# Last stage of a transformer block on Trainium2: second bias as matmul rows, shorter normalising passes, and the projection moved between turn and hidden layer

## What is computed

```python
x = x + conv_ref(_ln_c(x), Wq, bq, Wk, bk, Wv, bv, Wp, bp, rel_h, rel_w)   # attention; its last line is out @ Wp + bp
t = tokens(x)
t = t + ffn_ref(_ln_t(t), w1, b1, alpha_w1, alpha_a1, w2, b2, alpha_w2, alpha_a2)

def ffn_ref(x0, ...):
    xq = round(clip(x0 / alpha_a1.mean(), -8, 7))
    x1 = xq @ wq1.T * alpha_w1 * alpha_a1.mean() + b1
    x1 = clip(gelu(x1), -10, 10)
    hq = round(clip(x1 / alpha_a2.mean(), -8, 7))
    return hq @ wq2.T * alpha_w2 * alpha_a2.mean() + b2
```

## Time and profile before

| | us |
|---|---|
| median of 3 runs | 906.96 (906.38 to 907.9) |
| the profiled execution, its own time | 904.3 |
| span of its trace | 902.5 |
| busy in the span: TensorE | 791.0 (88%) |
| VectorE | 743.8 (82%) |
| ScalarE | 558.8 (62%) |
| POOL | 423.4 (47%) |
| mean granted TensorE clock, share of full speed | 0.949 |

### The profile page before, as it was taken

The page is one execution under the profiler, slowest core; times in us unless marked ns, Lnnn a source line. Parts: engine busy times, 40 slices in busy tenths (PEclk is TensorE's granted clock), DMA queues, the critical chain, the costliest instruction groups (busy, mean ns, idle before and its releaser), DMA issues. The chain is left out here.

```text
span 902.5 us, 15297 instructions
## 1 busy us (share of the span) xinstructions
PE 791.0 (88%) x5848; PEld 407.7 (45%) x5848; DVE 743.8 (82%) x1493; ACT 558.8 (62%) x609; POOL 423.4 (47%) x263
## 2 busy tenths in 40 slices
PE   5899554479999999999999999999999999678874
PEld 2555454134444444444444444444444442256653
DVE  6998855498989988988998999998888894069995
ACT  1333345027777777777777777777777778447773
POOL 3777794436364454637263735445373324112220
PEclk9999788589999999999999999999999999889986
DMA  7676599999439392948567493939395000433411
GB/s 193 212 226 206 164 300 374 256 194 208 90 88 188 77 200 60 205 85 190 111 147 154 109 191 74 198 68 201 63 206 96 13 12 12 134 105 123 140 36 53
DMA packets 65675, 130.06 MB, mean 144 GB/s; under 512 B 9465, under 2 KB 45306, under 8 KB 57146
## 3 DMA queue, kind: packets, MB, share of 16 engines
q1 hardware_dynamic: 57634, 115.95, 56.2%
q10 hardware_dynamic: 7968, 13.13, 4.2%
HBM read 89.73 MB, written 34.60 MB: 138 GB/s over the span
## 5 line engine op out<-in xcount | busy, mean ns | idle before, releaser
L1065 DVE TENSOR_REDUCE at_piece_neg<-at_r_ps 128x1 f32<-128x512 f32 x768 | 482.8, 682 | 68.1 <-PE at_r_ps L935 64.7
L1028 ACT ACTIVATE at_probs<-at_s_ps 128x1024 f32<-128x1024 f32 x384 | 371.9, 1021 | 130.6 <-PE at_s_ps L956 129.3
L935 PE MATMUL at_r_ps<-op_mix_k,op_mix_q 128*128 128x256 f16 (+1 forms) x1920 | 282.0, 257 | 29.9 <-DMA op_mix_q<-bias_parts 17.8
L935 PEld LDWEIGHTS at_r_ps<-op_mix_k,op_mix_q 128*128 128x128 f16 x1920 | 148.2, 98 | 295.1 <-DVE at_piece_neg L1065 194.1
L850 POOL COPY op_mix_q<-op_mix_q 2x4096 f16<-2x4096 f16 x48 | 172.6, 3596 | 231.0 <-ACT op_mix_q L1033 230.5
L956 PE MATMUL at_s_ps<-op_mix_q,op_mix_k 128*128 128x512 f16 x768 | 227.7, 380 | 1.1 <-ACT at_probs L1028 0.5
L970 PE MATMUL at_o_ps<-at_probs,op_v_u 128*32 128x512 f32 x1536 | 204.2, 604 | 0.0
L218 POOL MEMSET op_mix_q<- 2x10240 f32 x12 | 103.5, 8627 | 0.6
L1033 ACT ACTIVATE op_mix_q<-at_r_ps 2x1024 f16<-2x1024 f16 x48 | 48.5, 1011 | 60.7 <-PE at_r_ps L946 60.7
L956 PEld LDWEIGHTS at_s_ps<-op_mix_q,op_mix_k 128*128 128x128 f16 x768 | 73.4, 98 | 19.6 <-ACT at_probs L1028 10.7
L854 POOL TENSOR_TENSOR at_o_sb<-at_o_sb,at_inv_rows 128x512 f32<-128x512 f32 x24 | 30.7, 1280 | 86.2 <-DVE at_inv_rows L1092 86.2
(11 more groups left out here) (121 smaller groups left out, 674.4 us busy)
## 6 DMA issues: line engine op xcount, KB each, us to landing
op_mix_q<-qk_parts SPq DMA_DIRECT2D x48, 640.0 KB, 10.7
op_mix_q<-bias_parts SPq DMA_DIRECT2D x120, 120.0 KB, 10.3
op_mix_q<-bias_parts SPq DMA_DIRECT2D x72, 128.0 KB, 10.3
bias_parts<-op_mix_q ACTq DMA_DIRECT2D x8, 1024.0 KB, 13.1
qk_parts<-op_mix_q SPq DMA_DIRECT2D x24, 256.0 KB, 2.3
v_rows<-pr_v_st SPq DMA_DIRECT2D x8, 768.0 KB, 4.1
op_mix_k<-qk_parts SPq DMA_DIRECT2D x48, 128.0 KB, 13.1
op_v_u<-v_rows SPq DMA_DIRECT2D x12, 512.0 KB, 14.2
```

The lines of the kernel that those rows point to most:

```text
L935: last = pe.matmul(r_bank("piece", at)[:, first % GROUP:first % GROUP + n], mix_q[owner.buf][:, variant, j, qt * P:(qt + 1) * P], mix_k[ow ...
L1028: act.activation(probs[n % PRING][:, 2 * pair:2 * pair + 2, :], s_ps[pair][:, :, :], ACT.Exp).then_inc(exp_done, 1)
L1065: dve.tensor_reduce(piece_neg[half][:, i:i + 1], r_bank("piece", at)[:, :], AX_X, ALU.max, negate=True).then_inc(reduced, 1)
```

## The change

1. b2 is no longer added by VectorE. In `scales` it is divided by s2, split into three bf16 parts (high part, then the rest twice), and these go to rows 0, 32 and 64 of b2_parts, a bf16 tile of 96 rows, zero elsewhere. In `second` one more matmul per tile, a tile of ones against b2_parts, opens each sum in f_ps. `add_b2` and y_b go; b2 is loaded by `Weights.load`. y now has a ring of four buffers, and `residual` waits until the result four groups back is made.
2. `normalise`: POOL makes r0 * inv_a1 (r3) behind the power, and the third small operation takes it, so that y_n comes out divided by the activation's step. y_r is then (y_n + MAGIC) min (MAGIC + 7), and y_q is (y_r max (MAGIC - 8)) - MAGIC; y_i goes. The memset ahead of the statistics goes too.
3. `stage_c` scales all four tiles in one pass.
4. TensorE's `hidden` is split into `turn` and `hidden`, and the queue order is turn(g), project(g+2), hidden(g), second(g-1).

The diff, without the places that only pass b2 on:

```diff
-        self.dram = (w1, aw1, aa1, w2, aw2, aw2_cols, aa2)
+        self.dram = (w1, aw1, aa1, w2, aw2, aw2_cols, aa2, b2)
+        self.b2_parts = self.sb("b2_parts", [3 * SLOT, C], BF16)
+        self.ones = self.sb("ones", [3 * SLOT, P], BF16)
...
-        area, lens = ops.weight_area, (HT * C, HID, C, HT, HT)
+        area, lens = ops.weight_area, (HT * C, HID, C, HT, HT, C, C)
...
-        self.aa2_row, self.aa1_row, self.aw1_sb, self.inv_w1 = places[1:5]
+        self.aa2_row, self.aa1_row, self.aw1_sb, self.inv_w1, self.b2_row, self.inv_s2 = places[1:7]
+        self.b2_high = self.inv_s2.bitcast(BF16)[:, 0:C]
...
     def load(self, sp):
-        w1, aw1, aa1, w2, aw2, aw2_cols, aa2 = self.dram
...
+                         (self.aa1_row[:, :], aa1.partition_broadcast(P)), (self.aa2_row[:, :], aa2.partition_broadcast(P)),
+                         (self.b2_row[:, :], b2.partition_broadcast(P))):
             sp.dma_start(dst, src).then_inc(self.params_in, 16)
...
         step, link = self.step, lambda ins: self.chain(dve, ins)
-        dve.wait_ge(self.params_in, 16 * 7)
+        dve.wait_ge(self.params_in, 16 * 8)
         link(dve.reciprocal(self.inv_w1[:, :], self.aw1_sb[:, :]))
         link(dve.reciprocal(self.inv_w2[:, :], self.aw2_sb[:, :]))
         link(dve.tensor_reduce(step[:, 0:1], self.aa1_row[:, :], AX_X, ALU.add))
...
+        link(dve.memset(self.b2_parts[:, :], 0.0))
+        link(dve.memset(self.ones[:, :], 1.0))
+        link(dve.reciprocal(self.inv_s2[:, :], self.s2_row[:, :]))
+        link(dve.tensor_tensor(self.b2_row[:, :], self.b2_row[:, :], self.inv_s2[:, :], ALU.mult))
+        for i in range(3):
+            row = slice(i * SLOT, i * SLOT + 1)
+            link(dve.tensor_scalar(self.b2_high[:, :], self.b2_row[:, :], 1.0, None, ALU.mult))
+            link(dve.tensor_scalar(self.b2_parts[row, :], self.b2_high[row, :], 1.0, None, ALU.mult))
+            if i < 2:
+                link(dve.tensor_tensor(self.b2_row[:, :], self.b2_row[:, :], self.b2_high[:, :], ALU.subtract))
 
         for at, edge, limit, op in ((0, 10.0, QP, ALU.min), (1, -10.0, QN, ALU.max)):
             link(dve.tensor_scalar(self.bound[:, at:at + 1], self.inv_a2, edge, MAGIC, ALU.mult, ALU.add))
...
+    YRING = 4
...
-        y = [ph.sb(f"y{s}", [P, TILES, C], F32) for s in range(2)]
-        y_b = [ph.sb(f"y_b{s}", [P, TILES, C], F32) for s in range(2)]
+        y = [ph.sb(f"y{s}", [P, TILES, C], F32) for s in range(YRING)]
...
+        rstd = [ph.sb(f"rstd{s}", [P, 4, TILES], F32) for s in range(2)]
...
-        y_i = ph.sb("y_i", [P, TILES, C], BF16)
...
+                pool.wait_ge(pow_done, g.n + 1)
+                pool.tensor_tensor(out=rstd[g.s][:, 3, :], in0=rstd[g.s][:, 0, :], in1=wt.inv_a1.to_broadcast([P, TILES]), op=ALU.mult).then_inc(scaled_pow, 1)
 
             inverse_std(FIRST)
             inverse_std(FIRST.after(1))
...
-                st, mv, rs = stats[g.s], meanvar[g.s], rstd[g.s]
+                st, mv, y_g = stats[g.s], meanvar[g.s], y[g.n % YRING]
                 dve.wait_ge(x_loaded[g.s], (g.it + 1) * 16)
                 dve.wait_ge(proj_done, g.n + 1)
-                dve.tensor_tensor(y[g.s][:, :, :], p_ps[:, :, 0:C], x_in[g.s][:, :, :], ALU.add).then_inc(y_done, 1)
+                need(dve, res_done, g.n - YRING + 1)
+                dve.tensor_tensor(y_g[:, :, :], p_ps[:, :, 0:C], x_in[g.s][:, :, :], ALU.add).then_inc(y_done, 1)
                 dve.wait_ge(y_done, g.n + 1)
                 for t in range(TILES):
-                    last = dve.bn_stats(st[:, t, :], y[g.s][:, t, :])
+                    last = dve.bn_stats(st[:, t, :], y_g[:, t, :])
                 last.then_inc(stats_done, 1)
                 dve.wait_ge(stats_done, g.n + 1)
-                dve.memset(rs[:, 1, :], 0.0)
                 for t in range(TILES):
                     last = dve.bn_aggr(mv[:, t, :], st[:, t, :])
...
-                r0, r1, r2 = (rs[:, i, :] for i in range(3))
+                r0, r1, r2, r3 = (rs[:, i, :] for i in range(4))
                 dve.tensor_tensor(r1, r0, r0, ALU.mult).then_inc(newton, 1)
                 dve.wait_ge(newton, g.n * 3 + 1)
                 dve.scalar_tensor_tensor(out=r2, in0=r1, scalar=-0.5, in1=var_eps[g.s][:, :], op0=ALU.mult, op1=ALU.mult).then_inc(newton, 1)
                 dve.wait_ge(newton, g.n * 3 + 2)
-                dve.scalar_tensor_tensor(out=r1, in0=r2, scalar=1.5, in1=r0, op0=ALU.add, op1=ALU.mult).then_inc(newton, 1)
+                dve.wait_ge(scaled_pow, g.n + 1)
+                dve.scalar_tensor_tensor(out=r1, in0=r2, scalar=1.5, in1=r3, op0=ALU.add, op1=ALU.mult).then_inc(newton, 1)
                 dve.wait_ge(newton, g.n * 3 + 3)
                 for t in range(TILES):
-                    last = dve.tensor_scalar(y_n[:, t, :], y[g.s][:, t, :], mv[:, t, 0:1], rs[:, 1, t:t + 1], ALU.subtract, ALU.mult)
+                    last = dve.tensor_scalar(y_n[:, t, :], y[g.n % YRING][:, t, :], mv[:, t, 0:1], rs[:, 1, t:t + 1], ALU.subtract, ALU.mult)
                 last.then_inc(yn_done, 1)
                 dve.wait_ge(yn_done, g.n + 1)
 
-                dve.tensor_scalar(y_r[:, :, :], y_n[:, :, :], wt.inv_a1, MAGIC, ALU.mult, ALU.add).then_inc(yr_done, 1)
+                dve.tensor_scalar(y_r[:, :, :], y_n[:, :, :], MAGIC, MAGIC + QP, ALU.add, ALU.min).then_inc(yr_done, 1)
                 dve.wait_ge(yr_done, g.n + 1)
-                dve.tensor_scalar(y_i[:, :, :], y_r[:, :, :], MAGIC + QP, -MAGIC, ALU.min, ALU.add).then_inc(yi_done, 1)
-                dve.wait_ge(yi_done, g.n + 1)
                 need(dve, t_done, g.n - 1)
-                dve.tensor_scalar(y_q[g.s][:, :, :], y_i[:, :, :], QN, None, ALU.max).then_inc(yq_done, 1)
+                dve.tensor_scalar(y_q[g.s][:, :, :], y_r[:, :, :], MAGIC + QN, -MAGIC, ALU.max, ALU.add).then_inc(yq_done, 1)
 
             def stage_b(g, hf):
                 part = slice(hf * half_h, (hf + 1) * half_h)
...
 
             def stage_c(g):
                 dve.wait_ge(f_done, g.n + 1)
-                for t in range(TILES):
-                    last = dve.tensor_tensor(ffn[g.s][:, t, :], f_ps[:, t, 0:C], wt.s2_row[:, :], ALU.mult)
-                last.then_inc(scaled, 1)
+                dve.tensor_tensor(ffn[g.s][:, :, :], f_ps[:, :, 0:C], wt.s2_row[:, :].unsqueeze(1).to_broadcast([P, TILES, C]),
+                                  ALU.mult).then_inc(scaled, 1)
                 dve.wait_ge(scaled, g.n + 1)
-                dve.wait_ge(yb_done, g.n + 1)
                 need(dve, stored[g.s], g.it * 16)
-                dve.tensor_tensor(res[g.s][:, :, :], ffn[g.s][:, :, :], y_b[g.s][:, :, :], ALU.add).then_inc(res_done, 1)
-
-            def add_b2(g):
-
-                dve.wait_ge(y_done, g.n + 1)
-                need(dve, res_done, g.n - 1)
-                dve.tensor_tensor(y_b[g.s][:, :, :], y[g.s][:, :, :], b2_row[:, :].unsqueeze(1).to_broadcast([P, TILES, C]), ALU.add).then_inc(yb_done, 1)
+                dve.tensor_tensor(res[g.s][:, :, :], ffn[g.s][:, :, :], y[g.n % YRING][:, :, :], ALU.add).then_inc(res_done, 1)
 
             dve.memset(magic[:, :], MAGIC).then_inc(magic_made, 1)
             dve.tensor_scalar(lowest[:, :], wt.bound[:, 3:4], -MAGIC, None, ALU.add).then_inc(lowest_made, 1)
...
             normalise(FIRST)
             residual(FIRST.after(1))
-            add_b2(FIRST)
...
-                    add_b2(g.after(1))
 
             each_group(dve, emit)
             stage_c(LAST)
...
 
-            def hidden(g):
+            def turn(g):
                 pe.wait_ge(yq_done, g.n + 1)
                 need(pe, yt_ready, g.n)
                 for t in range(TILES):
                     for h in range(2):
                         last = pe.transpose(t_ps[0:HALF, h, t * P:(t + 1) * P], y_q[g.s][:, t, h * HALF:(h + 1) * HALF], ident[:, :])
                 last.then_inc(t_done, 1)
+
+            def hidden(g):
                 pe.wait_ge(yt_ready, g.n + 1)
                 for t in range(HT):
                     need(pe, gelu_done, g.n * HT + t - 2)
@@ -1460,8 +1465,9 @@
                 need(pe, scaled, g.n)
                 pe.wait_ge(hq_done, g.n * 2 + 2)
                 for t in range(TILES):
+                    pe.matmul(f_ps[:, t, 0:C], wt.ones[:, :], wt.b2_parts[:, :], start=True, stop=False)
                     for k in range(HT):
-                        last = pe.matmul(f_ps[:, t, 0:C], hid_q[g.s][:, k, t * P:(t + 1) * P], wt.w2_t[:, k, :], start=(k == 0), stop=(k == HT - 1))
+                        last = pe.matmul(f_ps[:, t, 0:C], hid_q[g.s][:, k, t * P:(t + 1) * P], wt.w2_t[:, k, :], start=False, stop=(k == HT - 1))
                 last.then_inc(f_done, 1)
 
             pe.wait_ge(ident_made, 1)
...
             project(FIRST.after(1))
 
             def emit(g):
-                hidden(g)
+                turn(g)
                 if not (g.last or g.after(1).last):
                     project(g.after(2))
+                hidden(g)
```

(37 more changed lines are left out.)

## The result

The changed kernel takes 931.05 us (median of 6 runs, 926.31 to 932.28), the kernel before, beside it, 907.35. The ratio is 1.0261, 95% interval 1.0243 to 1.0278: slower by 23.7 us. The forecast was slower, 924.8 us, with a range of 912 to 931, so the median lies just beyond its end.

What follows compares the result with a forecast made beforehand. VectorE's own queue was taken to bound the last stage, with the moved projection closing a loop. Last stage 6.3 + clock 6.8 + preparation 4.7 = +17.8 us on 906.96 gave 924.8 us, range 912 to 931.

Steps and rivals of the forecast that it cites:

- The loop: Last stage: clip, y, projection, hidden, gelu and hid_r wait in a circle; 13.0 us a group, +6.4 over five steps.
- The clock: TensorE in the last stage: idling before projections halves its granted clock, stretching projections 2 to 7; +6.8 us.
- four at 1.7: Four of projections 2 to 7 start at the low clock, each losing 1.7 us: +6.8 us.
- fourth rival: Last stage: every projection runs at the low clock, and longer, +14.4 us; total 932.4 us, chance 0.12.
- all six at 2.4: Upper bound for the low clock: each of projections 2 to 7 loses 2.4 us, 14.4 us in all.
- X(0): Start of group 0's first-half clip on VectorE, last stage; forecast at 810.4 us against 809.13, +1.3.
- second rival: TensorE's clock holds at full in the last stage, no low-clock cost; total 918.0 us, chance 0.15.
- VectorE's savings: Last stage: dropping add_b2, shorter y_i/y_q, one-pass scaling and no memset shed 1.6 us a group from VectorE.
- X(5) to X(6): From group 5's first-half clip to group 6's: no projection in the way, VectorE's 10.5 us, -1.6.
- Preparation: Twelve added VectorE instructions in scales, first stage, all on the path: +4.7 us.
- Head and end: Last stage: its start up to group 0's first-half clip +1.3 us; its tail, bias matmuls less quicker scalings, +0.2.
- X(6) to X(7): From group 6's first-half clip to group 7's: runs through y_q, turn, hidden and gelu as before, change 0.

Runs made afterwards that it cites:

- filler: The changed kernel with ten extra unused 512-column matmuls on TensorE between turn(g) and project(g+2), except for g = 0: 918.0 us, ratio 1.0133.
- residual_ahead: The changed kernel with residual(g+2) ahead of the first-half clip of group g in VectorE's queue: 903.26 us, ratio 0.9972.
- move_alone: The kernel before with only the projection moved between turn and hidden: 926.77 us, ratio 1.0237.

## Why the prediction was right and where it failed

**The loop: right.** Forecast: 13.0 us a step at the full clock, 9.08 of it beside the projection. Measured: 9.10 beside the projection in every step (16.11 - 7.01, 14.75 - 5.65, 16.04 - 6.94), and 13.07 a step with the filler. residual_ahead, which breaks the loop at one link, and move_alone, which has it without the rest of the change, show it as the cause.

**The clock: the term that was mis-sized.** The prediction took "four at 1.7", 6.8 us, of six projections. In the trace the term is 14.4: to hidden's start they took 5.66, 7.01, 5.65, 6.94, 5.65 and 6.91, 37.8 us against 6 x 3.90 = 23.4. Two things failed. First the count: all six met a low stretch, not four, which at 1.7 each adds 3.4. Second the length, and this is the reading of one row: the low stretch of 3.4 us behind the 1.42 us gap was taken as the usual one. Behind gaps of 2.85 us the low stretch was 3.4 us in one step, as assumed, and 6.8 in the next. Three projections cost 1.75 each and three 3.0 to 3.1, which adds the other 4.2.

That 14.4 is also the stated upper bound, and that the result lies near the fourth rival's 932.4 (chance 0.12), is in part luck. The bound was "all six at 2.4", and no projection cost 2.4. The price of a longer stretch had been read too low: the first projection of the kernel before began (785.59) in the midst of one. Its window, columns as in the earlier trace rows:

```profile
783.04:789.87 6.83, 4.28 (x13) 4.29 (x14) 0.16 (x2) 0.00 (x0) 0.59 (x4) 0.50 0.09 34
```

Only 4.3 of these 6.8 us fell on that projection. Besides, its busy time of 6.26 was set against 3.90 from start to start; against the busy time at the full clock, 4.07, it lost 2.2, half of 4.3. Read so, a stretch of 6.8 us wholly in dense work would cost 3.4, an estimate; the measured 3.0 to 3.1 have some 6 us of it.

The filler recovers 12.3 us between X(0) and X(5) in its trace (65.35 against 77.65).

**The rule of the Trainium skill** ("TensorE: Matmul & The Clock Gate", Part 1), weighed as the second rival: as I applied it, turn's transposes and the dense work on both sides would keep the clock. The trace disagrees with that reading: the clock fell in every one of these groups. It agrees with the rule's other half, that activity is what keeps the clock, as the filler shows.

**VectorE's savings: right in kind.** 1.6 us a group were forecast. The busy time of VectorE fell by 7.6 us in the whole kernel although the preparation adds 4.1, so by some 1.5 a group. With the order undone, this is worth 5.5 us in all, because TensorE's 11.27 then sets the pace; with residual_ahead the steps are 10.2 to 10.6. In the loop it is worth nothing but the step X(5) to X(6).

**Preparation: right.** Forecast 4.7, measured 4.6 and wholly on the path. Inside the sum errors cancel: the reciprocal took 1.35 and not 1.6, for which the slope of the medians (1.3) had been nearer than the steeper one, and the three conversions 0.9 and not 1.1, but the two memsets took 0.43 in place of 0.2 and the copies of a row 0.7 in place of 0.6.

**Head and end.** From projection 0 to X(0) the changed kernel took 3.3 us more (26.85 against 23.54), of which 1.75 are projection 2's low clock; the other 1.6 had been forecast as 1.3. The end was about as forecast: X(5) to X(6) took 10.4 us (forecast 10.5), X(6) to X(7) 8.75 in place of 9.0, the rest from X(7) 13.4 in place of 13.65 (0.2 more was forecast).

**The sum.** From the terms 6.3 + 14.4 + 4.6 = 25.3, against 23.7 between the medians. The 14.4 are those of the profiled execution, which is the slowest of the six. The two profiled executions differ by 28.0. Of this, 1.0 lies ahead of the first instruction of scales (36.47 against 35.49) and 2.2 between the second stage's start and the last stage's, in code that did not change. In the nine traces of this case, whichever the kernel, the first of these moments lies between 35.2 and 36.5, and the second stretch takes 683.3 to 686.1 us; so both look like scatter between single executions, as far as one trace of each kernel shows. Why the six times of the changed kernel fall into two clusters, 926.3 to 926.5 and 930.3 to 932.3, stays open.

## What to carry to other kernels

Before an instruction is moved ahead of others in an in-order queue, write down what it waits for, and follow that backwards through the other engines' queues: if the way leads through work that the moved instruction now delays, the step can't be shorter than the sum round the loop, however busy or idle each engine is. In this kernel the loop was charged twice, since its idle gap on TensorE lowered the clock for just the work that closes the loop. Two remedies break the loop: to move the projection back (904.75), or to bring its prerequisite forward on the other engine, residual ahead of the clip (903.26). They lie 1.5 us apart, and their intervals overlap. A second buffer for p_ps should break it too; that was not tried. The larger gain over them, some 5 us, came from putting one-time work where its engine waits anyway.

## What was not expected of the hardware

- The low clock after equal gaps lasted unequal times, 3.4 and 6.8 us in turn, in both kernels that have the loop without the filler (gaps of 2.85 us in the changed kernel, 3.19 in move_alone): the projection took 5.65 and then 6.9 us. After gaps of 0.6 to 1.9 us (filler, residual_ahead) it stayed high, while after the one of 1.42 in the kernel before it fell.
- Fifty useless matmuls of 512 columns, 2.3 us each ten, made the kernel 12 to 13 us faster.
- y_r on VectorE, the same pass of 128x768 in f32, takes 0.56 us with two constants (add, min) and took 0.62 with its scale read from a tile (multiply, add). Which of the two differences makes the 0.06 us was not tested.
